# Tail of an attention and mixture-of-experts block on one core: rows passed through in chunks, boundary terms in 32-column tiles, combine weights spread two ways

## The reference

```
x = x + conv_attention(ln_c(x))
    q, k, v = 8 heads of 16 channels; each token attends to 17 x 17 windows of k and v,
    in the unfold order of the reference (windows cross channels and heads);
    attn = softmax(q . k_windows) * mask; out = (attn . v_windows) @ w_proj.T + b_proj
t = tokens of x (1600 x 128)
t = t + moe(ln_t(t))
    logits = tokens @ router_w.T; probs = softmax; two best of 8 experts, weights divided by their sum
    out = tokens + sum over 8 experts of combine[:, e] * (gelu(tokens @ w1[e] + b1[e]) @ w2[e] + b2[e])
```

## Time and profile before

| | |
|---|---|
| median of 3 runs | 480.82 us (480.62 to 484.02) |
| the profiled execution | 485.29 us |
| its span, first to last instruction | 483.5 us |
| its mean granted TensorE clock | 0.883 |
| column loop ends, tail begins | about 342.5 us |
| last operation of an engine ends | 481.17 us |

### The profile page before, as it was taken

One profiled execution on the slowest core, in us unless ns is written; L12 is line 12 of the kernel. 1 busy time (PEld: TensorE's weight loads), 2 busy tenths in 40 slices (PEclk: granted clock), 3 DMA queues, 4 the chain that ended last, 5 costly groups with the idle time before them and its releaser, 6 DMA issues.

```text
span 483.5 us, 16599 instructions
## 1 busy us (share of the span) xinstructions
PE 438.1 (91%) x6970; PEld 306.9 (63%) x6970; DVE 319.2 (66%) x797; ACT 264.9 (55%) x465; POOL 194.3 (40%) x249
## 2 busy tenths in 40 slices
PE   4899937389899999999999999995899999999996
PEld 2789934157677777767766677774555545855553
DVE  1240173459999899989988889983387646264553
ACT  2240083948889998999999986862000000361332
POOL 9403044166866655556666786744000000001110
PEclk9785556779999999999999999999799757679999
DMA  6069995836666575767565654478640000007400
GB/s 195 21 217 292 212 298 175 275 89 212 198 207 204 205 235 170 225 220 218 193 216 187 207 173 161 176 206 225 225 68 0 2 0 0 1 0 272 157 17 35
DMA packets 39480, 77.24 MB, mean 160 GB/s; under 512 B 9412, under 2 KB 26453, under 8 KB 38589
## 3 DMA queue, kind: packets, MB, share of 16 engines
q1 hardware_dynamic: 38542, 74.61, 48.9%
q0 software_dynamic: 144, 1.36, 0.8%
q10 hardware_dynamic: 720, 0.22, 0.2%
HBM read 45.76 MB, written 29.29 MB: 155 GB/s over the span
## 4 chain that ended last, share of the span: by engine, by line
PE 82%; issue 8%; POOL 4%; DVE 3%; DMA 1%; ACT 1%; POOLq 0%; SPq 0%; DVEq 0%; ACTq 0%
PE ps L805 19%; PE ps L880 10%; PE ps L828 9%; PE ps L850 7%; PE ps L810 6%; PE ps L919 4%; PE ps L770 4%; PE ps L939 3%; PE ps L831 3%; PE ps L763 3%; PE ps L836 2%; PE ps L726 2%; PE ps L874 2%; PE ps L731 2%; PE ps L892 1%
## 5 line engine op out<-in xcount | busy, mean ns | idle before, releaser
L805 PE MATMUL ps<-slabs 128*32 128x401 f32 x528 | 119.5, 519 | 21.6 <-POOL slabs L529 20.4
L805 PE MATMUL ps<-prb,slabs 128*32 128x401 f32 x494 | 116.0, 522 | 0.0
L1064 DVE CUSTOM_DVE_ANT_0 scn<-ps,con 128x401 f32<-128x401 f32 x120 | 65.1, 571 | 35.1 <-PE ps L810 35.1
L670 ACT ACTIVATE exb<-scn,lowest 128x401 f32<-128x401 f32 x120 | 74.2, 621 | 11.3 <-DVE lowest L1064 11.2
L810 PEld LDWEIGHTS ps<-con,slabs 128*32 128x32 f32 x960 | 43.5, 113 | 50.0 <-issue 48.7
L1054 DVE COPY_PREDICATED slabs<-con,zt 128x1152 f32<-128x1152 int32 x41 | 67.2, 1640 | 0.1
L810 PE MATMUL ps<-con,slabs 128*32 128x128 f32 x960 | 62.7, 280 | 1.2 <-issue 1.1
L522 POOL TENSOR_TENSOR slabs<-con,qrot 128x192 f32<-128x192 f32 (+4 forms) x67 | 31.2, 468 | 80.8 <-DVE slabs L1054 76.1
L579 POOL TENSOR_TENSOR xln<-xln,wide 128x400 f32<-128x400 f32 x4 | 4.9, 1230 | 138.7 <-DVE wide L1228 138.7
L659 ACT ACTIVATE prb<-slabs 64x1169 f32<-64x1169 f32 x40 | 47.2, 1180 | 14.3 <-DVE slabs L1054 13.7
L587 ACT ACTIVATE prb<-wide 128x400 f32<-128x400 f32 x8 | 4.3, 537 | 87.6 <-DVE wide L988 87.3
(11 more groups left out here) (139 smaller groups left out, 757.5 us busy)
## 6 DMA issues: line engine op xcount, KB each, us to landing
slabs<-zsl SPq DMA_DIRECT2D x40, 539.5 KB, 4.0
zsl<-uv SPq DMA_DIRECT2D x44, 484.5 KB, 3.6
slabs<-combd SPq DMA_DIRECT2D x2, 1600.0 KB, 8.2
ebs<-zsl SPq DMA_DIRECT2D x4, 539.5 KB, 7.5
slabs<-kimd SPq DMA_DIRECT2D x2, 881.7 KB, 12.6
vimd<-vimg SPq DMA_DIRECT2D x1, 1612.0 KB, 5.7
xt<-x_in SPq DMA_DIRECT2D x8, 200.0 KB, 7.0
frd<-wide SPq DMA_DIRECT2D x2, 800.0 KB, 6.0
```

The source lines that it names most:

```text
L670: nc.scalar.activation(v(ex[x & 1], a, (1, NC3)), v(scn, (x & 1) * NB * NC3 + a, (1, NC3)), ACT.Exp, scale=-1.0, bias=lowest[:, NB * (x & ...
L805: mm(bank(g, (1, NC3), parts=TW, p0=TW * i), w, v((kt, kh)[b & 1][x & 1], b // 2 * C, (1, NC3)), start=first, stop=False, skip_group_check ...
L1064: nc.vector.tensor_tensor_reduce(v(scn, i * NC3, (1, NC3)), bank(g, (1, NC3)), cv("pos"), 1.0, 3e38, ALU.add, ALU.min, lowest[:, i:i + 1]) ...
```

## The change

Everything after the column loop is taken chunk by chunk, so that a chunk's later stages lie between the earlier stages of the next.

- SP writes `frot` in two parts (chunk 0, then the rest) and reads it back chunk by chunk, each with its semaphore.
- V's boundary terms. The 15 shifts of a chunk are four groups j of shifts j, j + 4, j + 8 and j + 12. One DVE instruction makes the products of a group (1600 elements, `product`); the last one or two groups of each chunk are made on POOL (`late_product`), from a copy of the permuted weights that ACT puts into SBUF (`copy_eb`). PE adds the shifts of a group into four different 32-column tiles of one bank (`vsum`), with the matrix `slot_of`, on top of the turned-back rows, which PE itself permutes into the bank first (`turned_back`). The rows of w_proj are permuted to the order in which the channels then lie. The first permutation of the boundary weights stands ahead of the last `products` of the loop, and DVE's first product and the reciprocals ahead of its last `pick_out`.
- The laying out of the reciprocals of the softmax sums moves from DVE to POOL (`rexp_rows`), and ACT copies their spread form to SBUF.
- Projection and centring are one accumulation: x times (identity - 1/C) plus the attention output times w_proj less its mean (`x_part`, `att_part`), both matrices made on DVE before the loop. ACT adds b_proj to x once, and squares and copies the centred chunk.
- Routing in three phases (chunk 0, chunk 1, chunks 2 and 3) of 17 links, with a tanh on ACT in place of the exponential and the division.
- The expert network: combine weights of chunks 0 to 2 spread by PE, of chunk 3 by DMA; its accumulation starts with the projection again (`y_start`), and POOL has added x and the normalised tokens before it (`start_sum`), so that one DVE addition ends a chunk. Register loops are written out.

```diff
+CT = Q // TT
+PHASES = ((0,), (1,), (2, 3))
+VGROUPS = 4
+VD = (3, 3, 2, 2)
+VQ = 8 * NCC
+NATB = (7, 6, 7, 7)
+PERMB = (0, 1, 2, 2)
+CENB = (0, 1, 2, 7)
+RNB = (4, 5, 4, 5)
+SMALL = ((4, 0, 32), (1, 416, 424), (2, 400, 408))
+COMBB = (4, 4, 2, 7)
+YB = 3
+BYPE = 3
...
+        mmat, wpm = wk, wv
+        cen = [uv[k // 2][:, k % 2 * Q:(k % 2 + 1) * Q] for k in range(NQ)]
+        sq = [v(slabs, 4 * L, (1, Q)), v(slabs, 4 * L, (1, Q)), pr[0][:, 0:Q], pr[0][:, Q:2 * Q]]
+        eb_late = [v(scn, 2 * Q + k * Q, (SZ, 10), (1, SZ), parts=VQ) for k in range(NQ)]
...
-                sp.dma_start(dv(frd, i * C * L, (L, C), (1, L)), frot[:]).then_inc(S["rot_out"], 16)
+            turn_out(0, 1, S["rot_first"])
+            turn_out(1, NQ, S["rot_out"])
...
+            def result(k):
+                sp.wait_ge(S["y_evac"], k + 1)
+                sp.dma_start(out[:, k * Q:(k + 1) * Q], fin[k]).then_inc(S["out_sent"], 16)
+
...
+            sp.wait_ge(S["vused_late"], vlate(NQ - 1, VGROUPS - 1) + 1)
+            sp.dma_start(v(slabs, 0, (1, E8 * Q)), dv(combd, 0, (0, C), (1, E8 * Q))).then_inc(weights_in, 16)
...
+            def late_product(k, j):
+                n, m = vlate(k, j), members(j)
+                pool.wait_ge(S["eb_out"], k + 1)
+                if n == 0:
+                    pool.wait_ge(S["av_done"], SZ)
+                    pool.wait_ge(S["gv_ready"], 1)
+                if n >= 2:
+                    pool.wait_ge(S["vused_late"], n - 1)
+                src = v(scn, 2 * Q + k * Q, (0, m), (SZ, 10), (1, SZ), parts=VQ)
+                gp.tensor_tensor(v(slabs, late_buf(n), (Q, m), (SZ, 10), (1, SZ), parts=VQ), src,
+                                 v(gv, j + 10 * k * PS, (VGROUPS, m), (PS, 10), (1, SZ), parts=VQ), ALU.mult
+                                 ).then_inc(S["vprod_late"], 1)
+
+            def start_sum(k):
+                pool.wait_ge(S["tokens"], k + 1)
+                gp.tensor_tensor(fin[k], xt[:, k * Q:(k + 1) * Q], xln[:, k * Q:(k + 1) * Q], ALU.add
+                                 ).then_inc(S["s_ready"], 1)
+
+            rexp_rows(0)
+            rexp_rows(1)
+            late_product(0, 3)
+            rexp_rows(2)
+            rexp_rows(3)
+            for k in range(1, NQ):
+                for j in range(VD[k], VGROUPS):
+                    late_product(k, j)
             for k in range(NQ):
-                pool.wait_ge(S["y_evac"], k + 1)
-                gp.tensor_tensor(xln[:, k * Q:(k + 1) * Q], xln[:, k * Q:(k + 1) * Q],
-                                 tok[:, k * Q:(k + 1) * Q], ALU.add).then_inc(S["y_sum"], 1)
...
+            def centred(k):
+                act.wait_ge(S["cen_ready"], k + 1)
+                if k == 1:
+                    act.wait_ge(S["cen_var"], 1)
+                nc.scalar.activation(sq[k], bank(CENB[k], (1, Q)), ACT.Square).then_inc(S["cen_sq"], 1)
+                nc.scalar.activation(cen[k], bank(CENB[k], (1, Q)), ACT.Copy).then_inc(S["cen_out"], 1)
+
+            def deviation(p):
+                t0, n = tiles_of(p)
+                act.wait_ge(S["cen_var"], PHASES[p][-1] + 1)
+                nc.scalar.activation(v(stat, t0, (1, n), parts=TT), bank(SMALL[p][0], (1, n), off=SMALL[p][1], parts=TT),
+                                     ACT.Sqrt, bias=epst[0:TT, 1:2]).then_inc(S["cen_std"], 1)
+
+            def second(p):
+                act.wait_ge(S["route"], NLINK * p + 8)
+                n = tiles_of(p)[1]
+                nc.scalar.activation(rt_(p, 8, (1, n)), rt_(p, 7, (1, n)), ACT.Tanh, scale=-0.5).then_inc(S["second"], 1)
...
+            copy_eb(0)
+            copy_eb(1)
+            copy_rn(0)
+            copy_eb(2)
+            copy_rn(1)
+            copy_rn(2)
+            centred(0)
+            copy_rn(3)
+            deviation(0)
+            act.wait_ge(S["w_late"], 112)
+            gelu(0, 0)
+            gelu(0, 1)
+            second(0)
+            copy_comb(0)
+            gelu(0, 2)
+            centred(1)
+            gelu(0, 3)
+            deviation(1)
+            gelu(0, 4)
+            gelu(0, 5)
+            copy_eb(3)
+            gelu(0, 6)
+            second(1)
+            gelu(0, 7)
+            centred(2)
+            centred(3)
+            copy_comb(1)
+            deviation(2)
+            for e in range(5):
+                gelu(1, e)
+            second(2)
+            for e in range(5, E8):
+                gelu(1, e)
+            copy_comb(2)
+            copy_comb(3)
+            for k in range(2, NQ):
                 for e in range(E8):
-                    gelu(k, e, 1)
+                    gelu(k, e)
...
+            def turned_back(k):
+                if k < 2:
+                    pe.wait_ge(S["masked"], SZ)
+                    pe.wait_ge(S["o_used"], SZ)
+                else:
+                    pe.wait_ge(S["att_nat"], (1, 3)[k - 2])
+                pe.wait_ge(nat_in[k], 16 * len(TURNED[k]))
+                mm(bank(NATB[k], (1, Q)), cv("perm"), v(sbd, k * Q, (1, Q)), start=True, stop=False, skip_group_check=True)
+
+            def vsum(k, j):
+                late = j >= VD[k]
+                if late:
+                    n = vlate(k, j)
+                    pe.wait_ge(S["vprod_late"], n + 1)
+                else:
+                    n = vgroup(k, j)
+                    pe.wait_ge(S["vprod"], n + 1)
+                for m in range(members(j)):
+                    n8 = live(j + VGROUPS * m)
+                    src = v(slabs, late_buf(n) + m * Q, (1, Q), parts=n8) if late else v(pr[n & 1], m * Q, (1, Q), parts=n8)
+                    last = mm(bank(NATB[k], (1, Q), parts=TW, p0=TW * m), cv("slot_of", (1, TW), off=24 - 8 * j, parts=n8), src,
+                              start=False, stop=(j + VGROUPS * (m + 1) >= HC - 1 and j >= 2), skip_group_check=True)
+                last.then_inc(S["vused_late" if late else "vused"], 1)
+
+            def x_part(k):
+                pe.wait_ge(S["xb_ready"], 1)
+                pe.wait_ge(S["late_mats"], 4)
+                if k < 3:
+                    pe.wait_ge(S["vprod"], (VD[0], VD[0] + VD[1], sum(VD))[k])
+                else:
+                    pe.wait_ge(S["att_nat"], NQ)
+                mm(bank(CENB[k], (1, Q)), mmat[:], xt[:, k * Q:(k + 1) * Q], start=True, stop=False, skip_group_check=True)
+
+            def att_part(k):
+                pe.wait_ge(S["att_nat"], k + 1)
+                mm(bank(CENB[k], (1, Q)), wpm[:], att[k], start=False, stop=True, skip_group_check=True
+                   ).then_inc(S["cen_ready"], 1)
+
...
+            def spread(k, e):
+                t = E8 * k + e
+                if e == 0:
+                    pe.wait_ge(S["route"], NLINK * (k + 1))
+                if t == 0:
+                    pe.wait_ge(S["att_nat"], 2)
+                elif e == 1 and k < 2:
+                    pe.wait_ge(S["comb_copied"], k + 1)
+                else:
+                    pe.wait_ge(S["weighted"], t - 1)
+                for i in range(CT):
+                    last = nc.tensor.transpose(bank((6, 4)[e & 1], (1, TT), off=TT * i),
+                                               v(lg, comb_at(k) + E8 * i + e, (0, C), parts=TT),
...
+                if i == SZ + 1:
+                    eb_rows(0)
...
+            eb_rows(1)
+            eb_rows(2)
+            rn_rows(0)
+            rn_rows(1)
+            turned_back(0)
+            vsum(0, 0)
+            vsum(0, 1)
+            turned_back(1)
+            vsum(0, 2)
+            vsum(0, 3)
+            x_part(0)
+            rn_rows(2)
+            vsum(1, 0)
+            att_part(0)
+            vsum(1, 1)
+            rn_rows(3)
+            variance(0)
+            vsum(1, 2)
+            rstd_rows(0)
+            logits(0)
...
+            up(0, 0)
+            up(0, 1)
+            turned_back(2)
+            vsum(2, 0)
+            x_part(1)
+            y_start(0)
+            spread(0, 0)
+            comb_rows(0)
+            y_bias(0)
+            spread(0, 1)
+
+            def step(k, e):
+                t = E8 * k + e + (3 if k else 2)
+                if t < E8 * NQ and (k or t < E8):
+                    up(t // E8, t % E8)
+                down(k, e)
+                if k < BYPE and e + 2 < E8:
+                    spread(k, e + 2)
+
+            step(0, 0)
+            att_part(1)
+            vsum(2, 1)
+            step(0, 1)
+            variance(1)
+            vsum(2, 2)
+            step(0, 2)
+            logits(1)
+            rstd_rows(1)
+            vsum(2, 3)
+            step(0, 3)
+            eb_rows(3)
+            turned_back(3)
+            step(0, 4)
+            vsum(3, 0)
+            vsum(3, 1)
+            step(0, 5)
+            vsum(3, 2)
+            vsum(3, 3)
+            step(0, 6)
+            x_part(2)
+            att_part(2)
+            step(0, 7)
+            x_part(3)
+            att_part(3)
+            for e in range(3):
+                up(1, e)
+            comb_rows(1)
```

(148 more changed lines are left out.)

419 lines of the change are left out of this document (193 added, 226 removed).

## The result

The changed kernel takes 513.5 us (median of 4 runs, 512.6 to 516.8) beside 481.3 us for the kernel before on the same chip: ratio 1.067, 95% interval 1.061 to 1.073, **slower**. The forecast was 468.2 with a range of 457 to 480. The profiled execution took 513.93 us, its span is 512.1. Some executions of a kernel are slower than its others at a lower granted clock; medians and ranges take in all of them, the ratios leave the slower ones out.

What follows compares the result with a forecast made beforehand. TensorE, busy 91% of the span, was taken to bind: 351 + 87.2 work + 19.0 waits gave span 460.2 with the ending; plus 2.0 POOL, 6.5 clock, 2.2 issue, 470.9, hence median 468.2; range 457 to 480.

Steps and rivals of the forecast that it cites:

- part 1: V's boundary sum in tiles: 60 full-width products (50.7 us) replaced by 16 groups, 11.5 us, plus four permutations, 2.7 us.
- rival 5: V's tiles aren't concurrent, four times 0.67 instead of once: adds 32 us, 500; chance 0.03 together with rival 3.
- The alternation with full-width products: Tiled groups alternating with full-width products some 24 times: taken at nothing, bound 0 to 0.2 us each, 0 to 5.
- rival 3: Each change between tiles and full width drains PE: 0.9 us each adds 21.6, 489.8; chance 0.03 together with rival 5.
- The clock: PE at half clock for 4 us around 351 (adds 4.0) and some 5 us behind later waits (adds 2.5).
- Rivals 2 and 4: PE at 1.2 GHz to chunk 0's end near 400, 478.6, chance 0.13; half clock through chunk 1, 489.3, chance 0.07.
- The start: PE waits for the turned-back rows (stores, gather) after three permutations: taken at 351, bounds 349 and 355.
- part 3: Chunks, from 351 to the end: PE's work 87.2 us at full clock plus waits of 19.0 us.
- POOL beside DVE: DVE's routing links slowed beside POOL's products: 0 to 8.7 us, taken at 2.0, ten links at 0.2 us more each.
- rival 6: POOL holds DVE for whole instructions, all 8.7 us instead of 2.0 come onto the path: 474.9; chance 0.07.
- Spreading: Combine weights of chunks 1 and 2 spread by PE instead of DMA: 16 times 0.35, 5.5 us dearer on PE's path.
- Tanh: Routing's tanh takes no table load of its own if in Gelu's tables; otherwise 5.4 us would show.

Runs made afterwards that it cites:

- e1: Changed kernel with V's shifts of 64 or fewer rows run on 120 rows, zero weights in the added rows: 474.12 us, ratio 0.982.
- e2: Changed kernel with V's sum by full-width 128-column weights, one product per shift, no tiles: 531.8 us.
- e6: Kernel of e1, but the third and fourth tile of each group on exactly 64 rows: 495.02 us, ratio 1.022.
- e3: Kernel of e1, with the turned-back rows of chunks 0 and 1 added after V's first groups: 470.32 us, ratio 0.976.
- e5: Kernel of e1 with the edits of both e3 and e4: 464.16 us, ratio 0.962.
- e4: Kernel of e1, with all sixteen grouped products on DVE and none on POOL: 469.35 us, ratio 0.973.
- e7: Kernel of e5, with chunk 3's combine weights spread by PE too instead of by DMA: 464.07 us, ratio 0.962.

## Why the prediction was wrong

**The step that failed is part 1, "16 groups at 0.67 to 0.72, together 11.5 us".** They took 53.0. The price was a row of tiles with 128 rows each, and the groups of this change mix rows of 104, 72, 40 and 8. e1, e2 and e6 show that products stand side by side only within a class of rows: 72, 104 and 120 go together, 64 and 64 go together, 40 and 8 do not. The boundaries lie between 72 and 64 and between 40 and 32, where the trace of before has its two stalls, and in the changed kernel the last group of a chunk, with 96, 64 and 32 rows, takes three steps (2.36 us at 423.05). This is rival 5 in kind ("the tiles aren't concurrent"), and it had got part of 0.03. It was priced at 32 us; unequal rows cost 36 us of PE's busy time over equal ones, of which 16 times 2.37 less 0.81, 25 us, are there at full clock and 11 come with the half clock. No rival reached 513.5: 500 was the slowest, and this loss and the clock's came together. The Trainium skill has the rule, on page TensorEngine Tiling (Array Packing), Key Properties: changing the tiling mode drains TensorE; and its Tiling Modes list 128, 64 and 32 rows as modes of their own. I had read the rule against the change between tiles and full width alone. By the runs it bears on the rows of a product, whatever its columns, 0.57 to 0.65 us of idle loading each time at full clock. Most of that idle time lies under the pair of passes that still runs (0.79 us a step beside 0.67); what is lost in the tiles is that the pairs don't overlap. In the trace of before the 0.57 us stood at 368.73 and 379.67, and I had not looked at single loads.

**The alternation with full-width products** was bounded at 0 to 5 us and taken at 0. It is in the upper half: in e1 a group takes 0.81 and the full-width pair behind it 0.87, both 0.67 without a change, 0.34 us together. Two groups in a row have it only once (1.47 us for 14 passes at 353.38 in e1), so there are 12 such places, the 24 changes of the forecast, and 12 times 0.34 is 4.1 us. At 0.17 a change the bound of 0.2 held, and rival 3's 0.9 each falls. The bound from the chain between L810 and L828 was the wrong witness for the value, since a busy PE hides the cost in the lengths of its own pieces.

**The clock** was put at 6.5 us, which is 13 us at 1.2 GHz. In the changed kernel the mean granted clock over the tail's 159.8 us is 0.82: 36% of that time is at 1.2 GHz, 58 us. In e1 it is 0.91 over 121.3 us, 22 us. Rivals 2 and 4 wanted half clock to last, and in part it did: 0.50 over 357 to 373 and over 382 to 398, though not through chunk 1's expert network (1.00 over 450 to 482). Equal rows took most of it away (e1 has 1.00 over 354 to 361), but e1 changes the serial steps and the row counts at once, and which of them the clock follows is not shown. Serial steps alone don't settle it: between full-width products the same three steps ran at 1.00 (409 to 428 in the changed kernel). Tiles aren't needed for it either: the kernel before had 0.50 over 380.4 to 404.3 with PE busy throughout, up to 400.7 on full-width products of 32 rows and fewer, and e2, without tiles, fell to 0.50 over 360 to 364 with PE busy.

**The start** held in the changed kernel: 351 foretold, 350.22 measured, and PE's wait is put down to the gather, 4.1 us. In e1 the same permutation came at 347.73, below the bound of 349, since that execution's loop ended 2.5 us earlier (its last pick at 339.99 beside 342.54). e3 and e5 agree that the wait lies open, e5's waits more clearly than the times.

**The rest of part 3** held as a sum. e1 is the changed kernel with that one error taken out, and its span is 471.9 against 470.9. That closeness is in part luck, since errors of both signs cancel. The start lay 3.3 us earlier. PE is busy for 103.8 us from 347.7 on, against 87.2 and 6.5, so 10.1 more: the alternations are 4.1 of it, and 22 us at 1.2 GHz cost up to 11 where 6.5 stood, up to 4.5 more. Its waits come to 17.5 us against 19.0 and the 4.2 for POOL and issue, 5.7 less. One wait looks mis-sized, 3.9 foretold before the fourth chunk's second group and 8.2 in e1, but 5.0 of it are the links that POOL held up: without POOL's products, in e4, it is 3.2.

**POOL beside DVE** was taken at 2.0 of up to 8.7 us. In e1's chain it is 5.0, and e4 gained 4.8 net of its own products: between the forecast and rival 6, which so was right in its mechanism. The price of 0.2 us for each link came from a misread row. The 0.78 us of the earlier trace rows is a mean over eight multiplications (not additions), of which most were not beside POOL at all; in the timeline of the kernel before, one of the two in the second line takes 1.41 us, the other 0.57 like those of the same form that stand clear of POOL:

```profile
446.02 1.30 POOL L579 TENSOR_TENSOR xln<-xln,wide 128x400 f32<-128x400 f32 x1 [108.44 <-DVE wide L1228]
446.34 2.00 DVE L1223 TENSOR_TENSOR scn<-kimg,slabs 128x400 f32<-128x400 f32 x2
```

In e1 DVE's link of 0.20 us lasted 2.69 under POOL's product, and ended with it. The Trainium skill, SBUF — State Buffer, section SBUF: two separate sides, has such a pair hold the port in turn for a whole instruction; this trace agrees, with those 2.69 us.

**Spreading** at 0.35 for an expert: 0.31 by e7. Chunks 2 and 3 came at 16.0 and 11.1 (15.3 and 10.9 foretold), and chunk 3 did not wait for its weights. Tanh took no table load. The six loads foretold are there: one at 326.59, before the first root, and five from 395 on; the kernel before has three.

## What to carry to other kernels

Before tiles of 32 columns are packed side by side, look at the rows of each. In these runs, whose rows are multiples of 8, products of 72 rows and more, of 40 to 64 and of 32 and fewer ran one after the other, and a zero-padded operand that brings them into one class is far cheaper (0.81 us for 2.37) than the shorter one. Take the price of packed tiles from a row of the trace whose tiles have the same shapes, and if there is none, bound it by all of them in series, at both clocks. Work that is moved to GpSimd to relieve VectorE is to be laid against VectorE's short chains of small operations, and not only against its long products.

## What the hardware showed that I had not expected

That the class of rows separates full-width products too (0.57 us of idle loading at each change at full clock, in e2 and in the kernel before). That the granted clock can fall with PE 100% busy in the trace (0.53 over 356 to 373, 17.00 of 17.00 us), so that each step costs 1.49 instead of 0.79 us; it was so in the kernel before too, on full-width products of few rows, and what the clock follows there is open. And that e1's longer operands cost nothing: its group of tiles on 104, 72, 120 and 120 rows, the last two with 40 and 8 rows that aren't zero, took 0.81 us, where each of the three steps of the changed kernel took 0.79.
